# Two attention passes of an image model: causal score slots rearranged, plain scores as float32r products on two row groups

## What is computed

```python
tokens = einsum('npi,di->npd', patches, W_map) + b_map     # class token ahead, positions added
x = (tokens - mean) / sqrt(var + eps) * ln_w + ln_b        # over tokens and channels of an image
q, k, v = ...                                              # per head, 16x16 weights
att = softmax(einsum('bshd,bthd->bhst', q, k) / sqrt(16))
h = tokens + einsum('bhst,bthd->bshd', att, v)             # first attention, no mask

q, k, v = (h @ W_qkv).reshape(..., 3, 12, 16)              # second attention
att = einsum('bhxd,bhyd->bhxy', q, k) * 16 ** -0.5
att = softmax(where(tril, att, -inf))
h = layernorm(h + att_times_v @ W_out + b_out)
...                                                        # 64 experts with soft routing, layernorm
```

## Time and profile before

| | |
|---|---|
| median of 3 runs | 4905.67 us (4903.66 to 4913.21) |
| the profiled execution: its time, its span | 4908.6 us, 4906.8 us |
| mean granted TensorE clock of the profiled execution | 0.96 |
| busy: TensorE, its weight loads, VectorE, ScalarE, POOL | 4504.7, 3888.5, 3050.0, 2746.9, 2724.9 us |
| VectorE's maxima, plain and causal (L770) | 798.4 and 642.3 us, 1536 each |
| exponentials, plain and causal (L713) | 638.8 and 512.3 us, 768 each |

### The profile page before, as it was taken

One profiled execution on the slowest core, in us unless ns is written; L12 is line 12 of the kernel. 1 busy time (PEld: TensorE's weight loads), 2 busy tenths in 40 slices (PEclk: granted clock), 3 DMA queues, 4 the chain that ended last, 5 costly groups with the idle time before them and its releaser, 6 DMA issues. The chain is left out here.

```text
span 4906.8 us, 161306 instructions
## 1 busy us (share of the span) xinstructions
PE 4504.7 (92%) x48311; PEld 3888.5 (79%) x48311; DVE 3050.0 (62%) x8728; ACT 2746.9 (56%) x6788; POOL 2724.9 (56%) x4491
## 2 busy tenths in 40 slices
PE   8999999899999999999979999999999788889964
PEld 8999999688888888888867777777777566669953
DVE  4555555566666666666556666666666599960057
ACT  3444444466666666666635555555555377764446
POOL 3444444466666666666656666666666488861135
PEclk9999999899999999999979999999999699999965
DMA  6777777677777777777656665665666133339978
GB/s 172 202 201 201 202 202 203 145 168 168 168 164 169 167 166 167 168 167 164 149 122 131 134 132 131 132 134 130 130 135 132 56 94 92 93 104 276 276 237 255
DMA packets 697918, 789.88 MB, mean 161 GB/s; under 512 B 367345, under 2 KB 519887, under 8 KB 697840
## 3 DMA queue, kind: packets, MB, share of 16 engines
q1 hardware_dynamic: 697840, 788.92, 66.1%
HBM read 519.30 MB, written 265.72 MB: 160 GB/s over the span
## 5 line engine op out<-in xcount | busy, mean ns | idle before, releaser
L770 DVE TENSOR_REDUCE a_mx<-a_sq 99x2 f32<-99x394 f32 x1536 | 798.4, 561 | 377.2 <-PE a_sq L821 376.9
L770 DVE TENSOR_REDUCE c_mx<-c_sq 99x2 f32<-99x198 f32 (+1 forms) x1536 | 642.3, 459 | 315.0 <-PE c_sq L821 314.7
L713 ACT ACTIVATE a_ex<-a_sk 99x792 f32<-99x792 f32 (+1 forms) x768 | 638.8, 832 | 106.6 <-PE a_sk L843 56.6
L713 ACT ACTIVATE c_ex<-c_sk 99x792 f32<-99x792 f32 (+1 forms) x768 | 512.3, 667 | 247.1 <-PE c_sk L837 173.9
L379 PE MATMUL e_tokp<-e_wmap,e_ptT 128*99 128x192 f32 x3072 | 544.3, 327 | 20.8 <-DVE e_cvar L332 20.8
L634 POOL TENSOR_SCALAR_AFFINE_SELECT c_ex<-c_ex 99x396 f32<-99x396 f32 (+1 forms) x768 | 422.0, 550 | 232.2 <-ACT c_ex L713 228.1
L379 PEld LDWEIGHTS e_tokp<-e_wmap,e_ptT 128*99 128x99 f32 x3072 | 483.2, 167 | 21.3 <-issue 20.8
L821 PE MATMUL a_sq<-a_ks,a_qs 96*99 96x198 bf16 x3072 | 441.5, 255 | 31.3 <-DMA a_ks<-scr_qk 16.4
L282 POOL CAST e_parts<-e_rest 96x396 bf16<-96x396 f32 x256 | 176.8, 691 | 483.1 <-DVE e_rest L338 483.1
L821 PE MATMUL c_sq<-c_ks,c_qs 96*99 96x99 bf16 (+1 forms) x3072 | 417.7, 231 | 0.0
L843 PE MATMUL a_sk<-a_qs,a_ks 99*99 99x198 bf16 (+1 forms) x3072 | 408.5, 254 | 3.0 <-issue 2.2
(11 more groups left out here) (196 smaller groups left out, 11487.7 us busy)
## 6 DMA issues: line engine op xcount, KB each, us to landing
e_ptT<-in_x SPq DMA_DIRECT2D x128, 594.0 KB
x_w<-in_fc SPq DMA_DIRECT2D x128, 576.0 KB, 5.8
scr_qk<-e_parts SPq DMA_DIRECT2D x128, 445.5 KB
scr_qk<-a_parts SPq DMA_DIRECT2D x128, 445.5 KB
scr_tv<-e_tv SPq DMA_DIRECT2D x128, 288.0 KB
a_tv<-scr_tv SPq DMA_DIRECT2D x128, 288.0 KB
scr_tv<-a_res SPq DMA_DIRECT2D x128, 288.0 KB
c_tv<-scr_tv SPq DMA_DIRECT2D x128, 288.0 KB
```

Source lines behind the costliest of these rows:

```text
L713: nc.scalar.activation(to, of, ACT.Exp).then_inc(exped.sem, 1)
L770: nc.vector.reduce_max(mx[:, b2.parity, qt, h:h + 2], sq[f % 2][:, :, 0:width], AX.X).then_inc(maxed.sem, 1)
```

## The change

**Plain pass, scores.** q and k become two float32r parts, high and rest, and each score is one product over 48 rows (high with high, high with rest, rest with high) or, with the maximum in two parts, 50. Heads 0 to 5 lie on rows 0 to 63 of the stacks, heads 6 to 11 on rows 64 to 127 (`half`). `shared_scores` writes the four key and the four query products of a slot alternately, and `heads_of` gives each fill a pair of heads on the other half than the key head beside it, so that consecutive products are on different row groups. The embed pass writes the two parts (no POOL work); the scratch array for them is 594 KB per image instead of 445.5 KB. SP loads q and k with eight transfers instead of six, and the maxima with four instead of three; POOL splits a maximum with two operations instead of four. The rows of ones in ks are now whole 32-row strips, filled by POOL (first thing in the pass) and VectorE before SP loads over parts of them.

**Causal pass.** Each slot's two fills are now one of the first query tile and one of the second (`heads_of`), and in slot 1 the turning of the maxima comes behind the value products of image c-5.

```diff
         xT = m.sb("e_xT", [CH + 1, 2, 2, SP])
-        rest = m.sb("e_rest", [CH, 2, 2, 2, SP])
...
-
-        @block.gpsimd
-        def _(pool):
-            for e in (middle, low):
-                e.seed(pool)
...
@@ -307,7 +285,7 @@
                 for i, (done, p) in enumerate(((q_done, qp), (k_done, kp))):
...
                 dve.wait_ge(high.sem, high.at(b3, i + 1))
-                dve.wait_ge(low.sem, low.at(b3 - 2, i + 1))
-                nc.vector.scalar_tensor_tensor(out=rest[:, b3.parity, i], in0=p[:], scalar=SCALES[i],
-                                               in1=parts[:, b3.place, i, :, place_of(i, 0)], op0=ALU.mult,
+                dve.wait_ge(stored.of(b3 - 4), stored.at(b3 - 4))
+                nc.vector.scalar_tensor_tensor(out=parts[:, b3.place, i, :, 1], in0=p[:], scalar=SCALES[i],
+                                               in1=parts[:, b3.place, i, :, 0].bitcast(F32), op0=ALU.mult,
...
+        def half(h):
+            return slice(64 * (h // HC), 64 * (h // HC) + 3 * DH), slice(64 * (h // HC), 64 * (h // HC) + 3 * DH + 2)
+
         def heads_of(fill):
-            return fill // 6, 2 * (fill % 6)
+            if not causal:
+
+                return ((0, 6), (1, 6), (0, 8), (1, 8), (0, 10), (0, 0), (1, 10), (1, 0), (0, 2), (1, 2), (0, 4), (1, 4))[fill]
+            return (fill % 2, 2 * (fill // 2)) if causal else (fill // 6, 2 * (fill % 6))
...
+                    else:
+                        if b.is_number(0):
+                            sp.wait_ge(ks_ones, 1)
+                            sp.wait_ge(ks_ones_above, 1)
+                        for c2 in range(2):
+                            for stack, i, at, of in ((qs, 0, 0, slice(0, 1)), (qs, 0, DH, slice(0, 2)),
+                                                     (ks, 1, 0, slice(0, 2)), (ks, 1, 2 * DH, slice(0, 1))):
+                                at += 64 * c2
+                                sp.dma_start(stack[at:at + (of.stop - of.start) * DH, b.place].rearrange("r h s -> r (h s)").bitcast(F32),
+                                             qk_in[b.number, i, c2, of].rearrange("a (d h) s -> (a d) (h s)",
+                                                                                  d=DH)).then_inc(qk_in_place.of(b), 16)
...
+                    else:
+                        for a in range(2):
+                            for c2 in range(2):
+                                at = 64 * c2 + 3 * DH + a
+                                sp.dma_start(qs[at:at + 1, b.place].bitcast(F32),
+                                             mxp[c2 * HC:(c2 + 1) * HC, b.parity, a].bitcast(F32)).then_inc(max_in_place.of(b), 16)
...
+            def ones_of_keys(of):
+                pool.memset(of, ONE_TWICE if causal else 1.0).then_inc(ks_ones, 1)
+                pool.wait_ge(ks_ones, 1)
+            if not causal:
+                ones_of_keys(ks[32:64].rearrange("p r h s -> p (r h s)").bitcast(F32))
             pool.memset(vx[:], 0.0).then_inc(zeroed, 1)
             pool.wait_ge(zeroed, 1)
...
+            def shared_scores(b4, b2, k):
+
+                g, kt = k // 2, k % 2
+                rows = TT - kt
+                if b4.inside(n):
+                    bank_of_keys(b4, k)
+                for j in range(G):
+                    f = 2 * k + j // 2
+                    if b4.inside(n):
+                        h = G * g + j
+                        mm = nc.tensor.matmul(sk[k % 2][0:rows, j // 2, (j % 2) * SP:(j % 2 + 1) * SP],
+                                              ks[half(h)[1], b4.place, h % HC, kt * TT:kt * TT + rows],
+                                              qs[half(h)[1], b4.place, h % HC], start=True, stop=True)
+                        if j == G - 1:
+                            mm.then_inc(scored_k.sem, 1)
+                    if b2.inside(n):
+                        qt, h = heads_of(f)
+                        h += j % 2
+                        if j % 2 == 0:
+                            bank_of_queries(b2, f)
+                        mm = nc.tensor.matmul(sq[f % 2][:, j % 2], qs[half(h)[0], b2.place, h % HC, qt * TT:(qt + 1) * TT],
+                                              ks[half(h)[0], b2.place, h % HC], start=True, stop=True)
+                        if j % 2:
+                            mm.then_inc(scored_q.sem, 1)
+
...
+                    if causal:
+                        if b4.inside(n):
+                            key_scores(b4, k)
+                        if b2.inside(n):
+                            query_scores(b2, 2 * k)
+                            query_scores(b2, 2 * k + 1)
+                    else:
+                        shared_scores(b4, b2, k)
...
-                    if k == 1 and b3.inside(n):
...
+                    if k == 1 and b3.inside(n) and not causal:
+                        turn_maxima(b3, b6)
...
                         if not causal:
                             pe.wait_ge(finished.sem, finished.at(b6 - 1))
                         value_products(b5, 2)
+                    if k == 1 and b3.inside(n) and causal:
+                        turn_maxima(b3, b6)
```

More of the change, by code:

```diff
@@ L485, in attend_pass @@
         ks_ones = m.sem(X + "ks_ones")
-        qk_in_place = m.transfers(X + "qk_in_place", 2 * PARTS)
+        ks_ones_above = m.sem(X + "ks_ones_above")
+        qk_in_place = m.transfers(X + "qk_in_place", 2 * PARTS if causal else 8)
         tv_in_place = m.transfers(X + "tv_in_place", 2)
@@ L495, in attend_pass @@
         max_low = m.event(X + "max_low")
-        max_in_place = m.transfers(X + "max_in_place", 3)
+        max_in_place = m.transfers(X + "max_in_place", 3 if causal else 4)
         v_spread = m.event(X + "v_spread")
@@ L559, in step @@
                     sp.wait_ge(max_low.sem, max_low.at(b))
-                    for a in range(PARTS):
-                        sp.dma_start(qs[STACK + a:STACK + a + 1, b.place], mxp[:, b.parity, a]).then_inc(max_in_place.of(b), 16)
+                    if causal:
+                        for a in range(PARTS):
+                            sp.dma_start(qs[STACK + a:STACK + a + 1, b.place], mxp[:, b.parity, a]).then_inc(max_in_place.of(b), 16)
+                    else:
[4 more added lines that the diff above has]
+                                             mxp[c2 * HC:(c2 + 1) * HC, b.parity, a].bitcast(F32)).then_inc(max_in_place.of(b), 16)
                 b = c - 2
@@ L599, in _ @@
             pool.wait_ge(vx_ones, 1)
-            pool.memset(ks[STACK:AUG].rearrange("p r h s -> p (r h s)").bitcast(F32), ONE_TWICE).then_inc(ks_ones, 1)
-            pool.wait_ge(ks_ones, 1)
+            if causal:
+                ones_of_keys(ks[STACK:AUG].rearrange("p r h s -> p (r h s)").bitcast(F32))
             if causal:
@@ L605, in max_parts @@
             def max_parts(b):
-                high, mid, low = (mxp[:, b.parity, a] for a in range(PARTS))
+                high, mid, low = (mxp[:, b.parity, a] for a in range(PARTS)) if causal else (mxp[:, b.parity, a] for a in (0, 0, 1))
                 of, left = mxn[:, b.parity], mxr[:, b.parity]
@@ L612, in max_parts @@
                 pool.wait_ge(max_high.sem, max_high.at(b))
+                if not causal:
+                    pool.tensor_tensor(low, of, high.bitcast(F32), ALU.subtract).then_inc(max_low.sem, 1)
+                    return
                 pool.tensor_tensor(left, of, high, ALU.subtract).then_inc(max_rest.sem, 1)
@@ L749, in _ @@
                 q_rest.seed(dve)
+            if not causal:
+                nc.vector.memset(ks[96:128].rearrange("p r h s -> p (r h s)").bitcast(F32), 1.0).then_inc(ks_ones_above, 1)
             if causal:
@@ L830, in key_scores @@
                 buf = sk[k % 2]
-                if k < 2:
-                    pe.wait_ge(exped.sem, exped.at(b - 1, 5 + k))
-                else:
-                    pe.wait_ge(exped.sem, exped.at(b, k - 1))
-                if causal and kt:
+                bank_of_keys(b, k)
+                if kt:
                     for j in range(G):
@@ L882, in tokens_times, with turn_maxima @@
                 mm.then_inc(done.sem, 1)
+            def turn_maxima(b3, b6):
+                pe.wait_ge(maxed.sem, maxed.at(b3))
+                pe.wait_ge(max_copied.sem, max_copied.at(b3 - 1))
+                if b6.inside(n):
+                    pe.wait_ge(h_low.sem, h_low.at(b6))
+                for t in range(2):
+                    mm = nc.tensor.transpose(mxT[:, t * TT:(t + 1) * TT], mx[:, b3.parity, t], ident[0:TT, 0:TT])
+                mm.then_inc(max_turned.sem, 1)
             def step(c):
@@ L887, in step @@
                     pe.wait_ge(ks_ones, 1)
+                    if not causal:
+                        pe.wait_ge(ks_ones_above, 1)
                     pe.wait_ge(vx_ones, 1)
```

84 lines of the change are left out of this document (42 added, 42 removed).

## The result

| | before | changed |
|---|---|---|
| median | 4909.44 us (4 runs, 4903.66 to 4924.45) | 5765.03 us (4 runs, 5759.98 to 5788.09) |
| ratio | | 1.1746, 95% interval 1.1704 to 1.1789 |
| profiled execution: time, span, mean granted clock | 4908.6, 4906.8, 0.96 | 5762.0, 5759.9, 0.75 |
| plain pass: first to last turning of the maxima, 127 steps | 922.8 to 2431.0, mean 11.88 | 928.2 to 3369.0, mean 19.22 |
| causal pass: the same | 2492.7 to 3822.8, mean 10.47 | 3451.5 to 4682.5, mean 9.69 |

The change is 17% slower; 4777 was forecast. The step times are worked out from the starts of the turnings of the maxima in the trace. 127 x (19.22 - 11.88) = +932 us in the plain pass, 127 x (9.69 - 10.47) = -99 in the causal one; the plain pass also drains some 19 us longer (35 to 54 us behind its last turning) and starts 4.6 later (first product at 913.3, now 917.9).

The account below looks back on a forecast made before the run. Both attention passes were taken to end on TensorE's queue at full clock. From 4908.6 us, -42 (plain), -93 (causal) and +4 (start) gave 4777.6, stated as 4777; forecast 4740 to 4815 (chance 0.48), wider range 4695 to 4870.

Parts of the forecast that it names:

- at granted clock 1.00: Opening step: TensorE bounds both attention passes, busy 59.50 of 60 us (plain) and 54.38 (causal) at full clock.
- The pair, 0.093: Plain-pass scores: two 198-column float32r products on different halves run together in 0.093 us, six slots 2.24 us.
- Rival 1: Plain-pass score slots: halves don't overlap, each pair 0.185 us, step +1.33, total about 4987, slower; chance 0.10.
- The switch, 0.155: Plain pass: each change between full height and 64 rows costs 0.155 us; nine more per step cost 1.40 us.
- Rival 2: Plain pass: every tiling switch drains TensorE fully, 0.23 us each, step 11.96, total 4824 or 4858; chance 0.14.
- The plain step 11.6: Plain pass: step falls from 11.93 to 11.6 us, waits for maxima included, giving -42 us over 126 steps.
- Four microseconds at the start: Start of plain pass: loads of q and k wait for a memset, +4 us once, range 0 to +6.
- The causal step 9.7: Causal pass: step falls from 10.44 to 9.7 us as two waits move, giving -93 us over 126 steps.
- Rival 3: Causal pass: maxima arrive late, step 10.0 to 10.2, pass gives only 30 to 55 us, total 4815 to 4840; chance 0.13.
- 0.6 and 0.15: Causal step: 0.6 us saved waiting for the low half of h, 0.15 waiting for the normalised output.

Follow-up runs that it names:

- the tiny products: Changed kernel with float32r plain scores at full height, plus one 16-column 64-row product ahead of each slot's key scores: 5023.64 us, step 13.56.
- The slot at full clock shown above: Timeline from the changed kernel with full-height bf16 filler products in the plain pass's first eight steps only: 4814.53 us, plain step 11.74.
- the pass kept at full clock (and with its fillers): Changed kernel, memsets cut by buffer, fillers ahead of the first score, in steps 2 to 4 and as a burst in step 7: median 4788.59 us, ratio 0.9752.
- the causal part alone: Kernel before with only the causal pass's even fills and moved turning of the maxima: 4799.25 us, ratio 0.9782.
- one kernel here: Changed kernel, memsets cut by buffer, fillers ahead of the first score and in steps 2 to 4, no step-7 burst: 4790.9 us, one run of six 5760.26.
- the blocked version: Changed kernel with each slot's four key products first, then its four query products, instead of alternating: 5763.25 us, step 19.47.

## Why the prediction was wrong

**The step that failed** is the first one, "at granted clock 1.00". All terms of the plain pass came from rows at that level, and the sum took for granted that the changed steps would run at it. No rival had the clock in it. The pass starts cold in both kernels; that the steps before raise the clock was a property of the work that the change replaced. One hint stood in view: the 64-row products of the combine pass run at 0.50. I used them for the overlap and scaled the clock away. It was a weak hint, since TensorE is busy only 51.59 of 100 us there, and the 64-row products of the route pass run at 1.00.

What the runs showed in its place: at full clock the plain step is 11.74 us, at half clock 19.41; in every trace this loop keeps the level that it meets. 126 x (19.41 - 11.74) = 966 of the 988 us between forecast and measurement.

The Trainium skill, "TensorE: Matmul & The Clock Gate", Part 1, says that the gate follows how busy the array has recently been and that activity releases it. The fall agrees: it comes where the embed pass runs dry (7.53 us busy of 10 in 890 to 900). The rise doesn't: 60.00 of 60 us busy at 0.50 in the changed kernel, 9.30 of 10 with the clock rising in the kernel before. The measurement decides: from the busy time of a profile one can't tell here whether the clock will rise.

**The other terms, at the clock they were meant for:**
- The pair, 0.093: 0.09. Rival 1 is out. What stood for it, reading at twice the rate of any row of the pass, was misread: the float32r projections read 96 rows in 0.092, a pair 98.
- The switch, 0.155: 0.15 by the tiny products. The slot at full clock shown above is near it: its first pair takes 0.17 us instead of 0.09, and the full-height product behind starts 0.19 after the last pair. Rival 2, the whole drain at 0.23, is out.
- The plain step 11.6: 11.74. Gain 0.2 per step instead of 0.33.
- Four microseconds at the start: 4.6.
- The causal step 9.7: 9.69. Rival 3, the maxima arriving late, shows only now and then. But the two reasons were shared out wrongly: 0.6 and 0.15 forecast, 0.74 and 0.1 measured. And the 0.15 named the wrong wait: the one for the normalised output did not shrink, while the wait of fills for maxima, forecast to grow, went.

With the pass kept at full clock (and with its fillers) the kernel takes 4788.59, 12 us from the forecast. That it comes so near is partly luck, since two misses cancel: the causal part alone gave 108 us where 93 were forecast, and the plain part, fillers included, 11 on top where 38 were forecast. So the prices of pair and switch were right, and the clock under them was not.

Open: why a step with all its scores on row groups doesn't raise the clock. It isn't the type, nor the gaps alone, nor row groups in half the slots. Whether it is the overlap of the halves or how much of the step lies on row groups, no run separates.

## What to carry to other kernels

Before pricing an edit on TensorE, ask at which clock the changed loop will start and whether its own work can raise it; a row at full clock is no price if the pass begins behind an idle stretch. Where a loop holds either level, a short burst of full-height products right ahead of it is cheap insurance; ahead of a wait and sparse steps it was lost again. Look at single runs too: one kernel here lost the clock in one run of six.

## What was not expected of the hardware

- The clock can stay at half for 2,400 us of back-to-back products, and for the rest of the pass at full after 10 us of other work.
- Products on different row groups start out of the program's order: in the blocked version a query product starts 0.01 us behind a key product, though three more key products stand ahead of it. So alternating them in the program bought nothing (19.41 against 19.47 at half clock; not run at full clock). The Trainium skill, "TensorEngine Tiling (Array Packing)", Key Properties, says that tiles operate independently; this agrees. The Trainium skill, "TensorE: Matmul & The Clock Gate", Part 3, says that products start strictly in program order; across the two row groups they don't here, and the measurement decides.
- Pairs of 198-column products are 0.167 us apart at half clock, which is 198 columns at 1.2 GHz (0.165), and 0.09 at full clock, where one full-height product alone takes 0.092: in the middle of a block neither the second half nor the load of its weights costs anything that shows.
